# P times V on a balanced array: heads 4 and 5 spread over four column groups, and one matmul chunk of the second MLP layer put ahead of the projection

## The chip, the cores and the metric

The kernel runs on one core of a Trainium2 chip. The core has five engines that run on their own and meet at semaphores: TensorE (PE, matmuls; the profile shows its weight loads apart, as PEld), VectorE (DVE), ScalarE (ACT), GpSimd (POOL) and SyncE (SP, which only issues DMAs here). Matmuls read SBUF and write PSUM; DVE and ACT carry results out of PSUM. The metric is the device time of one execution in microseconds, lower is better.

## What is computed

One Swin block on a batch of 16 images of 56 x 56 pixels with 192 channels, in float32: layer norm, shifted windows of 7 x 7 pixels, attention with 6 heads of 32 channels, projection, residual, layer norm, and an MLP with a hidden width of 768.

```python
xn = layernorm(x, ln1_w, ln1_b)
xs = jnp.roll(xn, shift=(-3, -3), axis=(1, 2))
xw = ...                                  # 1024 windows of 49 tokens
q, k, v = split(xw @ qkv_w + qkv_b)       # 6 heads of 32 channels
attn = softmax(einsum('bhqd,bhkd->bhqk', q, k) * scale)
o = einsum('bhqk,bhkd->bhqd', attn, v)    # P times V
x = x + unroll(o @ proj_w + proj_b)
h = gelu(layernorm(x, ln2_w, ln2_b) @ mlp_w1 + mlp_b1)
x = x + (h @ mlp_w2 + mlp_b2)
```

## The kernel before

The work is cut into 128 groups. A group is one row of 8 windows of one image, 392 tokens, and its 8 windows form 4 pairs. All engines run one loop over the groups, each with its own hand-written order (`body`), and the loop is software pipelined: in turn i, PE does the attention of group i, the MLP of group i-1 and the Q and K of group i+1. Large matmuls work on operands split into a high and a low part (zh and zl, oh and ol, gh and gl), so each evacuation from PSUM is two steps: ACT copies the high part out, then DVE subtracts it from the PSUM value to get the low part.

In one turn PE does, in this order: the scores `s` (L832), the transposes `transposes2` (L774, L776), the values `v` (L806 on zh and wqkv), the first MLP layer `mlp1` (L803), the transposed probabilities `turn_probs` (L910), `transposes1` (L766), two chunks of the second MLP layer `mlp2` (L878 to L884), P times V (`pv`, L929), mlp2 chunks 2 and 3 and the high part of chunk 4, the projection `proj` (L806 on oh, ol and wproj), the high part of chunk 5 and the low parts of 4 and 5, Q and K of the next group (`qk`, L803 on wqkv), and the transposes of the MLP result `turn_result` (L895, L898). A high part of a chunk is three matmuls (L878, L879, L880), a low part two (L883, L884).

P times V: for each of 4 pairs, 6 heads and 2 windows of the pair there is one matmul of a 49 x 32 stationary operand (values) and 49 moving columns (transposed probabilities), 48 in all. A float32 matmul stands in the trace as two weight loads and two matmuls, so 96 of each. The window of the pair sets the row half of the array (partitions 0 to 48 or 64 to 112), the head sets one of four groups of 32 columns, and so there are eight parts. Before the change, head h goes to column group h % 4: groups 0 and 1 carry two heads, groups 2 and 3 one. In program matmuls that is 8 for each of four parts and 4 for each of the other four; in trace records 16 and 8. The outputs of heads 0 to 3 lie in the first half of two PSUM banks, those of heads 4 and 5 in the second half, on 64 partitions.

After `pv`, ACT copies the high parts into oh: one instruction for heads 0 to 3 (L740, 128 partitions), one for heads 4 and 5 (L741, 64 partitions). DVE then makes the low parts (L584 into ol, L586 into the second half of oh), and `proj` waits for both (`ol_ready`). DVE goes on with the low parts of the next group's input (L433, L436), adds the residual to the projection (L530, one for each half, each after `proj_done`), takes statistics of it (L413, L418), moves queries out (L458), adds the narrow part of the MLP result (L548, `yTb_ready`), normalises (L426) and adds the second residual (L540, `yo_done`). `turn_result` on PE waits for L548 of the same turn; `v` of the next turn waits for L540, as `wait(pe, yo_done, 2, i - 2, 2)`, because the values go to the two PSUM banks that L540 reads. `s` waits for the copies of Q and K by ACT (L646, L649).

Of the kernel before, what the change touches and what calls it, by code (L numbers as in the profile page):

```python
# [7 lines left out]
ALU = mybir.AluOpType  # L8
ACT = mybir.ActivationFunctionType
AX = mybir.AxisListType  # L10
F32 = mybir.dt.float32
# [3 lines left out]
WS, SHIFT, HEADS = 7, 3, 6  # L15
HD = C // HEADS
TOK = WS * WS
# [3 lines left out]
PAIRS = WIN // 2  # L21
# [5 lines left out]
M = WIN * TOK  # L27
# [8 lines left out]
PROB_BLOCKS = ((0, 0), (0, 1), (4, 1), (1, 0), (1, 1), (5, 1), (2, 0), (2, 1), (4, 0), (3, 0), (3, 1), (5, 0))  # L36
# [3 lines left out]
def swin_kernel(nc, x, ln1_w, ln1_b, qkv_w, qkv_b, proj_w, proj_b, ln2_w, ln2_b, mlp_w1, mlp_b1, mlp_w2,  # L40
                mlp_b2, out):
    with ExitStack() as ctx:
# [42 lines left out]
        vt = sb("vt", [PAIR + 1, PAIRS, C])  # L85
# [4 lines left out]
        pt = sb("pt", [128, 2 * TILES, TOK])  # L90
        oh = sb("oh", [128, 2, M], F32R)
        ol = sb("ol", [128, M], F32R)
# [28 lines left out]
        PV = 2  # L121
# [59 lines left out]
        def wait(eng, s, per_group, group, k):  # L181

            v = group * per_group + k
            if not isinstance(v, int) or v > 0:
                eng.wait_ge(s, v)
# [26 lines left out]
        def by_window_parity(cols):  # L212

            return cols.rearrange("p (u w c) -> p w u c", w=2, c=WS)

        def outputs(part):

            return ps[:, PV:PV + 2, part * M // 2:(part + 1) * M // 2].rearrange("p w (u c) -> p w u c", c=WS)

        def half_of(t, half):  # L220

# [186 lines left out]
        def _(dve):  # L408
# [151 lines left out]
            def body(i, parity):  # L560
                prev = i - 1
                if attends(i):
                    scores(i, 0)
                if feeds(i):
                    low_wide2(prev)
                if attends(i):
                    scores(i, 1)
                if feeds(i):
                    low_narrow2(prev)
                if not feeds(i):  # L570
                    dve.wait_ge(consts_loaded, 16 * NCONST)
                    offset_bias(1, ((128, slice(HID0, HID0 + KC)),))
                if attends(i):
                    row_sums(i, 0)
                    row_sums(i, 1)
                    normalise(dve, i, 1)
                if more(i):
                    apply1(i + 1, 1 - parity)
                if more(i + 1) and attends(i):
                    stats1(i + 2, parity)  # L580
                if attends(i):

                    wait(dve, oh_ready, 2, i, 2)
                    dve.tensor_tensor(by_window_parity(ol[:, :]), outputs(0), by_window_parity(oh[:, 0, :]).bitcast(F32),  # L584
                                      ALU.subtract).then_inc(ol_ready, 1)
                    dve.tensor_tensor(by_window_parity(oh[64:128, 1, :]), outputs(1)[0:64],  # L586
                                      by_window_parity(oh[0:64, 1, :]).bitcast(F32), ALU.subtract).then_inc(ol_ready, 1)
                if more(i):
                    low_parts1(i + 1)
                if not feeds(i):  # L590
                    low_mlp_weights()
                if attends(i):

                    wait(dve, xb_done, 1, i, 1)
                    wait(dve, yo_done, 2, i - 2, 2)
                    wait(dve, z2_done, 1, i - 1, 1)
                    for half in range(2):
                        residual(i, parity, half)
                    wait(dve, x2_done, 2, i, 2)
                    norm_stats(x2[:, parity, :, :], st2, mv2, bn2, mv2_done, i)  # L600
                    if more(i):
                        queries_45(i + 1)
                if feeds(i):
                    narrow_result(prev)
                if attends(i):
                    z2_pieces = []
                    for h in range(BLOCKS // 2):
                        z2_pieces += [(z2[:, h, 0:C], 2 * h, slice(0, C)), (z2[:, h, C:C + B], 2 * h + 1, slice(A, C)),
                                      (z2[:, h, C + B:2 * C], 2 * h + 1, slice(0, A))]
                    wait(dve, t2_done, 1, i - 1, 1)  # L610
                    norm_apply(x2[:, parity, :, :], mv2, rs2, z2_pieces, i, mv2_done, rs2_done, z2_done)
                if feeds(i):
                    result(prev, 1 - parity)
# [5 lines left out]
        def _(act):  # L619
# [87 lines left out]
            def body(i, parity):  # L707
                prev = i - 1
                if feeds(i):
                    wait(act, h_done, KC, prev - 1, KC)  # L710
                    high_parts2(prev)
                if attends(i):
                    exponential(i, 0)
                    values(i)
                    exponential(i, 1)
                if feeds(i):
                    wait(act, spare_done, 2, prev - 1, 2)
                    act.activation(spare[:, :], ident[0:1, 0:1], ACT.Gelu).then_inc(spare_done, 1)
                    for m in range(4):
                        gelu(prev, m)  # L720
                    high_gelu(prev, 0)
                    high_gelu(prev, 1)
                if attends(i):
                    wait(act, pv_done, 1, i - 1, 1)
                    for half in range(2):
                        wait(act, pt_done, 2, i, half + 1)
                        act.activation(half_of(pt, half).rearrange("p (r s) q -> p r s q", r=2),  # L727
                                       ps[:, TP[half]:TP[half] + 2, 0:384]
                                       .rearrange("p r (s t) -> p r s t", t=64)[:, :, :, 0:TOK],
                                       ACT.Copy).then_inc(pt_ready, 1)  # L730
                if feeds(i):
                    high_gelu(prev, 2)
                    gelu(prev, 4)
                    gelu(prev, 5)
                    for m in range(3, KC):
                        high_gelu(prev, m)
                if attends(i):
                    wait(act, proj_done, 2, i - 1, 2)
                    wait(act, pv_done, 1, i, 1)
                    act.activation(by_window_parity(oh[:, 0, :]), outputs(0), ACT.Copy).then_inc(oh_ready, 1)  # L740
                    act.activation(by_window_parity(oh[0:64, 1, :]), outputs(1)[0:64], ACT.Copy).then_inc(oh_ready, 1)  # L741
                if more(i):
                    wait(act, v_done, 1, i, 1)
                    high_parts1(i + 1)
                if feeds(i):
                    wait(act, spare_done, 2, prev, 1)
                    act.activation(spare[:, :], ident[0:1, 0:1], ACT.Exp).then_inc(spare_done, 1)
                    narrow_result(prev)
                    wide_result(prev)
                else:  # L750
                    high_mlp_weights()
                    act.wait_ge(bias_ready, 2)
                if more(i):
                    keys_45(i + 1)
                    heads_0123(i + 1)
# [5 lines left out]
        def _(pe):  # L761
# [153 lines left out]
            def pv(i):  # L915

                wait(pe, pt_ready, 2, i, 2)
                pe.nop(nofuse=True)
                for pp in range(2):
                    for e in range(2):  # L920
                        for heads in ((0, 1, 4, 2), (3, 5)):
                            for h in heads:
                                b, p = PROB_BLOCKS.index((h, pp)), 2 * pp + e
                                cols = slice(32 * (h % 4), 32 * (h % 4) + 32)
                                for w in range(2):
                                    r = slice(64 * w, 64 * w + TOK)
                                    dst = ps[cols, PV + w, h // 4 * M // 2:(h // 4 + 1) * M // 2]\
                                        .rearrange("p (r q c) -> p q r c", q=PAIRS, c=WS)[:, p]
                                    last = pe.matmul(dst, vt[r, p, HD * h:HD * h + HD], pt[r, 2 * b + e, :], start=True,  # L929
                                                     stop=True)  # L930
                last.then_inc(pv_done, 1)

            def proj(i):
# [27 lines left out]
            def body(i, parity):  # L961
# [28 lines left out]
                    pv(i)  # L990
                if feeds(i):
                    mlp2(prev, (2, 3), (2, 3))
                    mlp2(prev, (4,), ())
                if attends(i):
                    proj(i)
                if feeds(i):
                    mlp2(prev, (5,), (4, 5))
                if more(i):
                    qk(i + 1, (2,))
                    qk(i + 1, (1, 0))  # L1000
# [24 lines left out]
```

## Time and profile before

| | us |
|---|---|
| median of 3 runs | 3045.3 |
| lowest and highest | 3044.94, 3047.61 |
| the profiled execution, its own time | 3046.47 |
| its span in the trace | 3044.7 |

| engine | busy us | share of the span |
|---|---|---|
| PE | 2996.3 | 98% |
| PEld | 2857.5 | 94% |
| DVE | 2376.0 | 78% |
| ACT | 2306.3 | 76% |
| POOL | 1483.4 | 49% |

The profile shows one execution. A busy share is the time in which an engine has an instruction running; matmuls overlap and their ends are modelled, so a PE that is never idle in this measure can still start its next matmul late. The starts of weight loads show that better: each load starts as soon as the matmul ahead of it has started, unless it waits for a semaphore.

### The profile page before, as it was taken

To read this page: it belongs to the slowest core of one execution; us is meant where nothing else is said; L and a number is where in the kernel's file an instruction comes from. 1 tells how busy PE (TensorE), PEld (TensorE's weight loads), DVE (VectorE), ACT (ScalarE), POOL (GpSimd) and SP (SyncE) were. 2 spreads that over 40 slices of the span, in tenths; PEclk is the share of its full clock that TensorE was granted. 3 is DMA by queue.
4 is the path that set the end of the run, shared out by engine and by line. 5 is a ranking of instruction groups with operands and counts; after the bars stand their busy time and mean duration, and the time that the engine had idled before them with its cause. 6 is when DMAs were issued, how large, how long until landed. Compare 5 with 4: busy or idle time off the path is not lost.

```text
span 3044.7 us, 114197 instructions
## 1 busy us (share of the span) xinstructions
PE 2996.3 (98%) x43444; PEld 2857.5 (94%) x43444; DVE 2376.0 (78%) x6416; ACT 2306.3 (76%) x4493; POOL 1483.4 (49%) x1550
## 2 busy tenths in 40 slices
PE   5999999999999999999999999999999999999998
PEld 5999999999999999999999999999999999999997
DVE  4778877887887788788778878877887788788775
ACT  2777777777777777777777777777777777777776
POOL 1454455445445544544554454445445544544553
PEclk7999999999999999999999999999999999999999
DMA  1000100010011001001100100010010001001100
GB/s 46 26 24 24 29 26 24 25 30 24 24 27 28 24 24 31 25 24 27 29 24 24 30 26 24 26 29 24 24 29 26 24 26 29 24 24 28 28 24 17
DMA packets 112145, 79.78 MB, mean 26 GB/s; under 512 B 10128, under 2 KB 111602, under 8 KB 112114
## 3 DMA queue, kind: packets, MB, share of 16 engines
q1 hardware_dynamic: 112114, 79.35, 9.7%
q8 instruction: 22, 0.36, 0.1%
q14 instruction: 9, 0.07, 0.0%
HBM read 40.78 MB, written 38.54 MB: 26 GB/s over the span
## 4 chain that ended last, share of the span: by engine, by line
PE 97%; SPq 1%; DVE 1%; ACT 0%; issue 0%; POOL 0%; DMA 0%; DVEq 0%; POOLq 0%; ACTq 0%
PE ps L803 35%; PE ps L806 16%; PE ps L878 6%; PE ps L910 5%; PE ps L832 5%; PE ps L883 5%; PE ps L929 4%; PE ps L884 4%; PE ps L880 4%; PE ps L879 4%; PE ps L766 3%; PE ps L774 2%; PE ps L895 2%; PE ps L898 1%; SPq L286 1%; PE ps L776 1%
## 5 line engine op out<-in xcount | busy, mean ns | idle before, releaser
L383 POOL TENSOR_TENSOR gl<-g,gh 128x392 fp32r<-128x392 f32 x768 | 789.5, 1050 | 251.6 <-ACT gh L668 251.3
L803 PE MATMUL ps<-zh,w 128*128 128x392 f32 x3072 | 715.0, 348 | 0.6 <-ACT zh L630 0.6
L803 PEld LDWEIGHTS ps<-zh,w 128*128 128x128 f32 x3072 | 533.9, 189 | 31.4 <-ACT zh L630 0.8
L263 POOL TENSOR_TENSOR prob<-prob,rcp 128x588 f32<-128x588 f32 x128 | 152.2, 1189 | 537.0 <-DVE rcp L558 537.0
L413 DVE BATCH_NORM_STATS2 st<-xin 98x6 f32<-98x192 f32 x512 | 145.8, 348 | 328.1 <-DMA xin<-in_x 327.9
L662 ACT ACTIVATE g<-ps,biasf 128x392 f32<-128x392 f32 x768 | 389.3, 574 | 3.1 <-PE ps L803 3.0
L366 POOL TENSOR_TENSOR xb<-xin,projbv 98x768 f32<-98x768 f32 x128 | 234.5, 1832 | 296.2 <-DVE z L426 266.2
L803 PE MATMUL ps<-zh,wqkv 128*128 128x400 f32 x1536 | 378.1, 355 | 0.0
L668 ACT ACTIVATE gh<-g 128x392 fp32r<-128x392 f32 x768 | 365.1, 533 | 0.0
L803 PEld LDWEIGHTS ps<-zh,wqkv 128*128 128x128 f32 x1536 | 289.9, 190 | 2.5
L806 PE MATMUL ps<-wqkv,zh 128*114 128x192 f32 x2048 | 289.5, 269 | 0.4 <-issue 0.4
L878 PE MATMUL ps<-gh,w2h 128*128 128x392 f32 x768 | 288.8, 376 | 0.2 <-ACT pt L727 0.2
L680 ACT ACTIVATE yn<-ps,b 64x392 f32<-64x392 f32 x128 | 74.7, 583 | 279.0 <-PE ps L884 279.0
L376 POOL TENSOR_TENSOR rs<-ve,mhalf 98x4 f32<-98x4 f32 x256 | 259.8, 1015 | 20.1
L374 POOL TENSOR_TENSOR ve<-mv,eps 98x4 f32<-98x4 f32 x256 | 51.7, 202 | 445.4 <-DVE mv L418 445.4
L883 PE MATMUL ps<-gl,w2h 128*128 128x392 f32 x768 | 262.8, 342 | 0.1
L803 PE MATMUL ps<-zl,w 128*128 128x392 f32 x768 | 262.6, 342 | 0.0
L806 PEld LDWEIGHTS ps<-wqkv,zh 128*114 128x114 f32 x2048 | 257.2, 181 | 5.5 <-issue 0.5
L884 PE MATMUL ps<-gl,w2s 128*128 128x392 f32 x768 | 261.8, 341 | 0.0
L880 PE MATMUL ps<-gh,w2s 128*128 128x392 f32 x768 | 261.7, 341 | 0.0
L879 PE MATMUL ps<-gh,w2l 128*128 128x392 f32 x768 | 260.7, 339 | 0.0
L806 PE MATMUL ps<-wproj,oh 128*98 128x192 f32 x2048 | 251.3, 253 | 2.3 <-DVE oh L586 2.3
(105 smaller groups left out, 7234.2 us busy)
## 6 DMA issues: line engine op xcount, KB each, us to landing
xin<-in_x SPq DMA_DIRECT2D x128, 147.0 KB
out<-yo SPq DMA_DIRECT2D x128, 147.0 KB
xin<-in_x SPq DMA_DIRECT2D x128, 71.2 KB
out<-yo SPq DMA_DIRECT2D x128, 71.2 KB
xin<-in_x SPq DMA_DIRECT2D x128, 54.8 KB
out<-yo SPq DMA_DIRECT2D x128, 54.8 KB
xin<-in_x SPq DMA_DIRECT2D x128, 18.8 KB
out<-yo SPq DMA_DIRECT2D x128, 18.8 KB
```

The source lines that it names most:

```text
L366: pool.tensor_tensor(xb[:, parity, :, :], xin[:, parity, :, :], projbv[:, :].unsqueeze(1).broadcast_to([PART, BLOCKS, C]), ALU.add)\
L376: pool.tensor_tensor(rs[:, :], ve[:, :], mhalf[:, :], ALU.pow).then_inc(rs_done, 1)
L383: pool.tensor_tensor(gl[:, m, :], g[:, m, :], gh[:, m, :].bitcast(F32), ALU.subtract)\
L662: act.activation(g[:, m, :], ps[:, H[m], 0:M], ACT.Gelu, bias=biasf[:, HID0 + m:HID0 + m + 1])\
L668: act.activation(gh[:, m, :], g[:, m, :], ACT.Copy).then_inc(gh_done, 1)
L803: last = pe.matmul(dst, cols(w, part), act_ if zh is zh2 else windows(act_, WIDE, EVEN), start=(n == 0), stop=(n == 4))
L806: last = pe.matmul(dst, act_[:, tokens], cols(w, part), start=(n == 0), stop=(n == 4))
L878: pe.matmul(wide, w2h[:, k, :], gh[:, k, :], start=(k == 0), stop=False)
L879: pe.matmul(wide, w2l[:, k, :], gh[:, k, :], start=False, stop=False)
L880: pe.matmul(narrow, w2s[:, k, :], gh[:, k, :], start=(k == 0), stop=False)
L883: pe.matmul(wide, w2h[:, k, :], gl[:, k, :], start=False, stop=(k == KC - 1))
L884: last = pe.matmul(narrow, w2s[:, k, :], gl[:, k, :], start=False, stop=(k == KC - 1))
```

## The change

Three edits.

1. In `pv`, heads 4 and 5 of even pairs stay on column groups 0 and 1, those of odd pairs go to groups 2 and 3. Each of the eight parts then gets 6 program matmuls, 12 in trace records. The order within `pv` is changed too: for each two pairs, heads 0 to 3 of the one, heads 0 to 3 of the other, and then heads 4 and 5 of both. The number and shape of the matmuls stay.
2. The outputs of heads 4 and 5 now lie on 128 partitions, half as wide. They are still brought to the same place in oh for the projection, so the copy L741 becomes two copies (one for each parity of pairs, 64 partitions x 196 elements), and so does the subtraction L586. DVE waits for three copies in place of two.
3. The high part of mlp2 chunk 5 moves from behind `proj` to ahead of it.

```diff
--- before.py
+++ after.py
@@ -213,9 +213,17 @@
 
             return cols.rearrange("p (u w c) -> p w u c", w=2, c=WS)
 
-        def outputs(part):
-
-            return ps[:, PV:PV + 2, part * M // 2:(part + 1) * M // 2].rearrange("p w (u c) -> p w u c", c=WS)
+        def outputs_0123():
+
+            return ps[:, PV:PV + 2, 0:M // 2].rearrange("p w (u c) -> p w u c", c=WS)
+
+        def outputs_45(e):
+
+            return ps[64 * e:64 * e + 64, PV:PV + 2, M // 2:M // 2 + M // 4].rearrange("p w (u c) -> p w u c", c=WS)
+
+        def pairs_of_parity(cols, e):
+
+            return cols.rearrange("p (u e w c) -> p e w u c", e=2, w=2, c=WS)[:, e]
 
         def half_of(t, half):
 
@@ -580,11 +588,14 @@
                     stats1(i + 2, parity)
                 if attends(i):
 
-                    wait(dve, oh_ready, 2, i, 2)
-                    dve.tensor_tensor(by_window_parity(ol[:, :]), outputs(0), by_window_parity(oh[:, 0, :]).bitcast(F32),
-                                      ALU.subtract).then_inc(ol_ready, 1)
-                    dve.tensor_tensor(by_window_parity(oh[64:128, 1, :]), outputs(1)[0:64],
-                                      by_window_parity(oh[0:64, 1, :]).bitcast(F32), ALU.subtract).then_inc(ol_ready, 1)
+                    wait(dve, oh_ready, 3, i, 3)
+                    dve.tensor_tensor(by_window_parity(ol[:, :]), outputs_0123(),
+                                      by_window_parity(oh[:, 0, :]).bitcast(F32), ALU.subtract).then_inc(ol_ready, 1)
+                    for e in range(2):
+                        hi, lo = slice(64 * e, 64 * e + 64), slice(64 - 64 * e, 128 - 64 * e)
+                        last = dve.tensor_tensor(pairs_of_parity(oh[lo, 1, :], e), outputs_45(e),
+                                                 pairs_of_parity(oh[hi, 1, :], e).bitcast(F32), ALU.subtract)
+                    last.then_inc(ol_ready, 1)
                 if more(i):
                     low_parts1(i + 1)
                 if not feeds(i):
@@ -737,8 +748,10 @@
                 if attends(i):
                     wait(act, proj_done, 2, i - 1, 2)
                     wait(act, pv_done, 1, i, 1)
-                    act.activation(by_window_parity(oh[:, 0, :]), outputs(0), ACT.Copy).then_inc(oh_ready, 1)
-                    act.activation(by_window_parity(oh[0:64, 1, :]), outputs(1)[0:64], ACT.Copy).then_inc(oh_ready, 1)
+                    act.activation(by_window_parity(oh[:, 0, :]), outputs_0123(), ACT.Copy).then_inc(oh_ready, 1)
+                    for e in range(2):
+                        act.activation(pairs_of_parity(oh[64 * e:64 * e + 64, 1, :], e), outputs_45(e), ACT.Copy)\
+                           .then_inc(oh_ready, 1)
                 if more(i):
                     wait(act, v_done, 1, i, 1)
                     high_parts1(i + 1)
@@ -916,18 +929,27 @@
 
                 wait(pe, pt_ready, 2, i, 2)
                 pe.nop(nofuse=True)
+                def head_of(h, pp, e):
+
+                    b, p = PROB_BLOCKS.index((h, pp)), 2 * pp + e
+                    for w in range(2):
+                        r = slice(64 * w, 64 * w + TOK)
+                        if h < 4:
+                            dst = ps[32 * h:32 * h + 32, PV + w, 0:M // 2].rearrange("p (r q c) -> p q r c", q=PAIRS, c=WS)[:, p]
+                        else:
+                            c0 = 64 * e + 32 * (h - 4)
+                            dst = ps[c0:c0 + 32, PV + w, M // 2:M // 2 + M // 4]\
+                                .rearrange("p (r q c) -> p q r c", q=2, c=WS)[:, pp]
+                        last = pe.matmul(dst, vt[r, p, HD * h:HD * h + HD], pt[r, 2 * b + e, :], start=True, stop=True)
+                    return last
+
                 for pp in range(2):
                     for e in range(2):
-                        for heads in ((0, 1, 4, 2), (3, 5)):
-                            for h in heads:
-                                b, p = PROB_BLOCKS.index((h, pp)), 2 * pp + e
-                                cols = slice(32 * (h % 4), 32 * (h % 4) + 32)
-                                for w in range(2):
-                                    r = slice(64 * w, 64 * w + TOK)
-                                    dst = ps[cols, PV + w, h // 4 * M // 2:(h // 4 + 1) * M // 2]\
-                                        .rearrange("p (r q c) -> p q r c", q=PAIRS, c=WS)[:, p]
-                                    last = pe.matmul(dst, vt[r, p, HD * h:HD * h + HD], pt[r, 2 * b + e, :], start=True,
-                                                     stop=True)
+                        for h in range(4):
+                            head_of(h, pp, e)
+                    for e in range(2):
+                        for h in range(4, HEADS):
+                            last = head_of(h, pp, e)
                 last.then_inc(pv_done, 1)
 
             def proj(i):
@@ -990,11 +1012,11 @@
                     pv(i)
                 if feeds(i):
                     mlp2(prev, (2, 3), (2, 3))
-                    mlp2(prev, (4,), ())
+                    mlp2(prev, (4, 5), ())
                 if attends(i):
                     proj(i)
                 if feeds(i):
-                    mlp2(prev, (5,), (4, 5))
+                    mlp2(prev, (), (4, 5))
                 if more(i):
                     qk(i + 1, (2,))
                     qk(i + 1, (1, 0))
```

In the order of the changed kernel line numbers are 8 to 14 higher (L878 becomes L891, L883 L896, L806 L819, L929 L943, L584 L592, L586 L596). PE between P times V and the next Q and K, first before (two chunks of mlp2, of which the last row of chunk 3 is shown, then the high part of chunk 4, the projection, the high part of chunk 5):

```order
L884 MATMUL ps<-gl,w2s 128x392
L878 MATMUL ps<-gh,w2h 128x392
L879 MATMUL ps<-gh,w2l 128x392
L880 MATMUL ps<-gh,w2s 128x392
L806 MATMUL ps<-wproj,oh 98x192 x2
L806 MATMUL ps<-wproj,ol 98x192
...
L806 MATMUL ps<-wproj,oh 98x192 x2
L878 MATMUL ps<-gh,w2h 128x392
L879 MATMUL ps<-gh,w2l 128x392
L880 MATMUL ps<-gh,w2s 128x392
L883 MATMUL ps<-gl,w2h 128x392
```

The same place now:

```order
L897 MATMUL ps<-gl,w2s 128x392
L891 MATMUL ps<-gh,w2h 128x392
L892 MATMUL ps<-gh,w2l 128x392
L893 MATMUL ps<-gh,w2s 128x392
L891 MATMUL ps<-gh,w2h 128x392
L892 MATMUL ps<-gh,w2l 128x392
L893 MATMUL ps<-gh,w2s 128x392
L819 MATMUL ps<-wproj,oh 98x192 x2
L819 MATMUL ps<-wproj,ol 98x192
...
L819 MATMUL ps<-wproj,oh 98x192 x2
L896 MATMUL ps<-gl,w2h 128x392
```

Three matmuls moved from behind the projection to ahead of it; nothing else on PE changed places but the order inside `pv`.

DVE around the low parts of the attention output, before:

```order
L413 BN_STATS st<-xin 98x6 x4
L418 BN_AGGR mv<-st 98x2 x4
L584 TENSOR_TENSOR ol<-ps,oh 128x2x28x7
L586 TENSOR_TENSOR oh<-ps,oh 64x2x28x7
L433 TENSOR_TENSOR zl<-ps,zh 128x8x49
L436 TENSOR_TENSOR zh<-ps,zh 64x8x49
L530 TENSOR_TENSOR x<-ps,xb 98x384 x2
```

And now:

```order
L421 BN_STATS st<-xin 98x6 x4
L426 BN_AGGR mv<-st 98x2 x4
L592 TENSOR_TENSOR ol<-ps,oh 128x2x28x7
L596 TENSOR_TENSOR oh<-ps,oh 64x2x14x7 x2
L441 TENSOR_TENSOR zl<-ps,zh 128x8x49
L444 TENSOR_TENSOR zh<-ps,zh 64x8x49
L538 TENSOR_TENSOR x<-ps,xb 98x384 x2
```

One subtraction became two of half the width; the place is the same.

## Rows read from the trace of the kernel before

**Rows 1.** The page: busy us, share of the span, instructions.

```profile
PE 2996.3 (98%) x43444; PEld 2857.5 (94%) x43444; DVE 2376.0 (78%) x6416; ACT 2306.3 (76%) x4493; POOL 1483.4 (49%) x1550
```

**Rows 2.** DVE in order of time: start, length, what, idle before.

```profile
1502.44 0.57 DVE L584 TENSOR_TENSOR ol<-ps,oh 128x392 fp32r<-128x392 f32 x1 [0.86 <-ACT oh L741]
1503.03 0.56 DVE L586 TENSOR_TENSOR oh<-ps,oh 64x392 fp32r<-64x392 f32 x1
...
1504.23 0.57 DVE L436 TENSOR_TENSOR zh<-ps,zh 64x392 fp32r<-64x392 f32 x1
1504.94 0.56 DVE L530 TENSOR_TENSOR x<-ps,xb 98x384 f32<-98x384 f32 x1
1505.73 0.56 DVE L530 TENSOR_TENSOR x<-ps,xb 98x384 f32<-98x384 f32 x1 [0.24 <-PE ps L806]
1506.33 1.14 DVE L413 BATCH_NORM_STATS2 st<-x 98x6 f32<-98x192 f32 x4
...
1507.98 0.85 DVE L458 TENSOR_SCALAR qB<-ps,biasf 64x200 f32<-64x200 f32 x2
1508.76 0.71 DVE L548 TENSOR_TENSOR yTb<-ps,yn 64x196 f32<-64x196 f32 x2
1509.50 1.63 DVE L426 TENSOR_SCALAR z<-x,mv,rs 98x192 f32<-98x192 f32 x6
1511.05 1.02 DVE L540 TENSOR_TENSOR yo<-ps,x 98x512 f32<-98x512 f32 x2
```

**Rows 3.** Weight loads (PEld) in order of time, ahead of projection, transposes and values.

```profile
1503.39 0.19 PEld L880 LDWEIGHTS ps<-gh,w2s 128*128 128x128 f32 x1
1503.65 0.27 PEld L806 LDWEIGHTS ps<-wproj,oh 128*98 128x98 f32 x2
...
1509.08 0.38 PEld L803 LDWEIGHTS ps<-zh,wqkv 128*128 128x128 f32 x2
1509.54 0.46 PEld L895 LDWEIGHTS ps<-ident,yT 128*98 128x98 f32 x4
...
1511.85 0.23 PEld L776 LDWEIGHTS ps<-ident,z 98*128 98x128 f32 x2
1512.12 0.28 PEld L806 LDWEIGHTS ps<-wqkv,zh 128*114 128x114 f32 x2
```

**Rows 4.** The transposes' load in a later turn, DVE and then PEld.

```profile
2506.29 0.71 DVE L548 TENSOR_TENSOR yTb<-ps,yn 64x196 f32<-64x196 f32 x2
...
2507.07 0.46 PEld L895 LDWEIGHTS ps<-ident,yT 128*98 128x98 f32 x4
```

**Rows 5.** The chain of waits in order of time: start, length, what.

```profile
1500.32 1.07 PE ps L929 x73
...
1506.07 0.18 PE ps L880
...
1510.47 1.15 PE ps L832 x71
```

**Rows 6.** P times V in the first turn and in a later one, PE in order of time.

```profile
58.29 1.62 PE L929 MATMUL ps<-pt,vt 49*32 49x49 f32 x96
...
1500.25 1.14 PE L929 MATMUL ps<-pt,vt 49*32 49x49 f32 x96
```

**Rows 7.** Windows of those two: stretch, us, busy PE, busy PEld, granted clock, DMA share, GB/s.

```profile
58.29:59.63 1.34, 1.34 (x95) 1.34 (x96) 0.50 0.31 69
1500.25:1501.31 1.06, 1.06 (x96) 1.00 (x96) 1.00 0.00 0
```

**Rows 8.** ACT in order of time: the copies after P times V, and a pair of half-width copies.

```profile
1501.48 0.53 ACT L740 ACTIVATE oh<-ps 128x392 fp32r<-128x392 f32 x1 [0.29 <-PE ps L929]
1501.90 0.50 ACT L741 ACTIVATE oh<-ps 64x392 fp32r<-64x392 f32 x1
...
1512.70 0.67 ACT L633 ACTIVATE zh<-ps 64x196 fp32r<-64x196 f32 x2
```

## The prediction

> **What bounds the kernel now.** The page comes first: PE is busy 98% of the span, its weight loads 94%, DVE 78%, ACT 76% [rows 1]. Read alone, it says that PE is the bound and the rest follows. The busy time of PE can't show a matmul that starts late, so I went to the starts of the weight loads and set them beside DVE in order of time [rows 2, 3]. Three loads a turn start late, and each has an instruction of DVE that ends just before it.
>
> The projection: the load ahead of it starts at 1503.39 and loads come every 0.18 us there, so it could start at 1503.57; it starts at 1503.65, and DVE's last low part (L586) ends at 1503.03 + 0.56 = 1503.59. It is 0.08 us late. The transposes of the MLP result: two loads of L803 from 1509.08 take 0.38, so 0.19 apart, and the next could start at 1509.46; it starts at 1509.54, and L548 ends at 1508.76 + 0.71 = 1509.47. Again 0.08 late. The values of the next turn: L540 ends at 1511.05 + 1.02 = 1512.07, the load starts at 1512.12, 0.27 after the last pair of L776 loads began and so about 0.1 later than a load that waits for nothing [rows 2, 3]. A turn 1000 us later has the same distance: L548 ends at 2506.29 + 0.71 = 2507.00, the load starts at 2507.07 [rows 4]. So these are waits that bind, each small.
>
> They belong to one loop. DVE's second residual add starts at 1505.73 after 0.24 of idling on PE, when the projection is done. From there DVE works without a pause that matters: 1506.33, 1507.98, 1508.76, 1509.50, 1511.05, to 1512.07 [rows 2]. That is 3.74 us to the end of L548 and 6.34 to the end of L540, whatever PE does meanwhile. PE spends the 3.74 on what stands behind the projection: mlp2 chunks, Q and K. It fills them all but 0.08. **The work between the projection and the transposes is PE's cover for DVE, and it is used up on both sides.** A turn is as long as PE's way from the values to the end of the projection, plus DVE's way from there to the values.
>
> **The change part by part.** There are 127 turns with all the pieces (a first without an MLP, a last without attention); one takes 23.2 us.
>
> The moved chunk. Three matmuls go from behind the projection to ahead of it, 0.18 each [rows 5], 0.54 us. Ahead of the projection they first fill its wait of 0.08. The rest, 0.46, makes the projection end later. Behind it PE comes to the transposes 0.54 earlier, and L548 is not a bit earlier: it comes 3.74 after the second residual add starts, and that add waits for the projection. So the wait at L895 grows from 0.08 to 0.62, and the turn by 0.54 - 0.08 = 0.46 us. The moved loads need the high part of chunk 5, which ACT makes before it copies the output of P times V; ACT even idles 0.29 before that copy [rows 8], so this waits for nothing. Late next, once the transposes wait longer: the scores, the next MLP's transposes and the values. The values wait for L540, which stays 2.60 behind L548 (1512.07 - 1509.47), as before; the scores' wait for the copies of Q and K only becomes easier.
>
> The copies in two. ACT's second copy, L741, takes 0.50; a pair of half width, L633, takes 0.67 [rows 8]: +0.17. DVE's L586 takes 0.56; a pair of half width, L548, takes 0.71 [rows 2]: +0.15. The access patterns are different (runs of 7 elements), so the ends are 0 and, if each half cost a full one, 0.50 + 0.56 = 1.06; I take 0.32, the pair rows being of the same size in elements. They lie on the way from P times V to the projection. That way had no slack (0.08 too long); with 0.54 us more PE work beside it there is 0.46, and 0.32 fits. **The split costs nothing, but only since the chunk was moved.** Queued behind the two subtractions are L433, L436 and the first residual add. L436 would end at 1504.80 + 0.32, the add at 1504.94 goes with the projection to + 0.46, so 0.28 of idling remains there; nobody waits.
>
> P times V. The chain gives it 1.07 us [rows 5]. Its fullest parts have 16 of the 96 matmuls, and after the change 12. If the fullest part sets the time, it falls to 12/16 of 1.07 = 0.80: a gain of 0.27. Against that, two sets of rows. The scores have the same number, 96 records, evenly over eight parts, 12 each, and take 1.15 [rows 5]; their stationary operand has 64 columns for 32, but if balance were the key they would not be slower than the uneven one. And the first turn ran at half clock (0.50, that is 1.2 GHz, against 1.00 or 2.4 GHz later) [rows 7]: P times V took 1.62 there and 1.14 at full clock [rows 6], 1.4 times and not 2. So at full clock most of it is not bound by the array's own streaming, but by something that does not follow that clock; 96 pairs in 1.07 are 11 ns a pair, the scores' 12 ns. I take the pace at which pairs are handed to the array as the bound, which balance does not change. The bounds are a gain of 0.27 and a loss of 0.08 (the scores' pace); I take a gain of 0.03, near to the scores' row, for the spells in which a part is asked for twice in a row.
>
> In TensorEngine Tiling (Array Packing) the Trainium skill says, under Key Properties, that tiles operate independently and can load weights and multiply in parallel. By that rule the fullest part is the bound and the gain is the 0.27 above; the half-clock rows and the scores speak against it as the bound at full clock, and it stands as a rival below.
>
> Sum: 0.54 - 0.08 - 0.03 = 0.43 us a turn, x127 = 55 us. On the span of 3044.7 that is 3100, on the execution's own 3046.5 it is 3101, on the median of 3045.3 it is 3100. **I forecast 3100 us, 1.8% slower.**
>
> **Rivals.**
>
> A. The fullest part of the array is the bound. P times V gains 0.27 in place of 0.03: (0.46 - 0.27) x 127 = 24 us, 3069. Still slower: the gain in P times V is real, but less than what the moved chunk exposes. For it: 16 turns of the fullest part in 1.07 are 67 ns each, a plausible load and stream. Against it: the scores and the half clock. Chance 0.20.
>
> B. It gets faster. PE is the bound after all, and the order behind the projection is free: the DVE work has slack that the trace doesn't show. Then the 0.08 at the projection goes, with 0.03 to 0.27 of P times V: 0.11 x 127 = 14 us, 3031, down to 0.35 x 127 = 44 us, 3001. It decides at the transposes: it holds if DVE's way to L548 shrinks by over 0.46 when PE runs ahead. Against it: loads that start 0.07 after L548 a thousand us apart, and a DVE without pauses from the second add on. Chance 0.08.
>
> C. It stays within the noise: A, and DVE's way gets some 0.2 shorter. 3045. Chance 0.03.
>
> D. The split copies cost far more than the pairs suggest, up to a full copy each, 1.06. Then the projection waits for L596 again: 1.06 - 0.46 = 0.60 more, (0.43 + 0.60) x 127 = 131 us, 3176. It decides from 0.46. The pair rows speak against it: 0.32. Chance 0.05.
>
> **How the numbers follow.** The forecast has 0.64, A 0.20, B 0.08, C 0.03, D 0.05. The predicted time is 3100. The range takes in A with its bound, 3067, and at the upper end P times V at the scores' pace: (0.46 + 0.08) x 127 = 69, 3114. These hold 0.84 less what falls just outside. A measurement of this kernel can tell some 0.2%, 6 us, from no change. Faster by more than that: B, 0.08. Within it: 0.03. Slower: 0.64 + 0.20 + 0.05 = 0.89.
>
> **What would show each step right or wrong.** The chunk: the load of L908 (the transposes) would start some 0.6 after the last load of Q and K in place of 0.27, still 0.07 behind DVE's narrow result, and PE's busy share would fall for the first time by a visible amount. The second residual add would still be followed by 3.74 us to the end of the narrow result. The projection: its first load would come 0.18 behind the load ahead of it, and DVE's last low part would have ended 0.1 to 0.2 earlier. P times V: 1.04 in the chain, where A says 0.80. The copies: 0.67 for ACT's pair, 0.71 for DVE's. I am wrong if the load of the transposes starts without a wait, or if the turn is 23.2 us or less; the step that failed would then be the length of DVE's way.

## The result and the profile after

The changed kernel took 3109.07 us in the median of 4 runs (3107.56 to 3110.56), the kernel before beside it 3046.45 (3044.94 to 3047.64): a ratio of 1.0208, 95% interval 1.0196 to 1.0220. It is slower, by 63 us or 0.49 us a turn. I had forecast 3100, in a range of 3067 to 3114.

The first lines of the page of the changed kernel, as [rows 1]:

```profile
span 3108.8 us, 114514 instructions
...
PE 3024.9 (97%) x43444; PEld 2852.8 (92%) x43444; DVE 2396.4 (77%) x6544; ACT 2344.9 (75%) x4621; POOL 1482.8 (48%) x1550
```

PE's busy time rose by 29 us with the same 43444 instructions, while the weight loads' fell by 5 us, to 92% of the span from 94%. In Perfetto Trace Analysis, under Identifying the Most-Contended Engine, the Trainium skill says that the matmul busy share is not a good measure of how close a kernel is to its limit, and names the busy share of weight loads (and the share of peak arithmetic) in its place. This trace agrees: the time grew by 2%, the loads' share fell by two points and the matmuls' by one.

DVE in order of time in one turn of the changed kernel, from the low parts to the second residual of the MLP result, as [rows 2]:

```profile
1486.26 0.57 DVE L592 TENSOR_TENSOR ol<-ps,oh 128x392 fp32r<-128x392 f32 x1 [1.00 <-ACT oh L753]
1486.85 0.73 DVE L596 TENSOR_TENSOR oh<-ps,oh 64x196 fp32r<-64x196 f32 x2
...
1489.09 0.56 DVE L538 TENSOR_TENSOR x<-ps,xb 98x384 f32<-98x384 f32 x1 [0.31 <-PE ps L819]
1489.89 0.56 DVE L538 TENSOR_TENSOR x<-ps,xb 98x384 f32<-98x384 f32 x1 [0.24 <-PE ps L819]
...
1492.91 0.71 DVE L556 TENSOR_TENSOR yTb<-ps,yn 64x196 f32<-64x196 f32 x2
...
1495.21 1.01 DVE L548 TENSOR_TENSOR yo<-ps,x 98x512 f32<-98x512 f32 x2
```

The second residual add starts at 1489.89 and the narrow result (L556, L548 before) ends at 1492.91 + 0.71 = 1493.62, 3.73 later; the second residual of the MLP ends at 1496.22, 6.33 later. Before it was 3.74 and 6.34: DVE's way kept its length to 0.01 us.

The weight loads of the same turn, as [rows 3]:

```profile
1487.56 0.19 PEld L893 LDWEIGHTS ps<-gh,w2s 128*128 128x128 f32 x1
1487.73 0.34 PEld L819 LDWEIGHTS ps<-wproj,oh 128*98 128x98 f32 x2
...
1492.72 0.38 PEld L816 LDWEIGHTS ps<-zh,wqkv 128*128 128x128 f32 x2
1493.69 0.39 PEld L908 LDWEIGHTS ps<-ident,yT 128*98 128x98 f32 x4 [0.59 <-issue]
...
1496.27 0.28 PEld L819 LDWEIGHTS ps<-wqkv,zh 128*114 128x114 f32 x2
```

The load ahead of the projection (1487.73) comes 0.17 behind the one ahead of it and waits for nothing; the low part L596 had ended at 1487.58. The load of the transposes could start at 1493.10 and starts at 1493.69, 0.59 late and 0.07 after L556 ended. In [rows 3] it was 0.08 late, with the same 0.07. The values' load starts 0.05 after the second residual (L548) ended, as before (L540 there).

The copies on ACT, as [rows 8]:

```profile
1485.11 0.53 ACT L751 ACTIVATE oh<-ps 128x392 fp32r<-128x392 f32 x1 [0.26 <-PE ps L943]
1485.52 0.70 ACT L753 ACTIVATE oh<-ps 64x196 fp32r<-64x196 f32 x2
```

The pair of half-width copies takes 0.70 on ACT (I took 0.67), and 0.73 on DVE (0.71).

The chain of waits of the changed kernel in the same turn, and the projection of the next one, as [rows 5]:

```profile
1483.98 1.03 PE ps L943 x67
...
1488.07 1.78 PE ps L819 x20
...
1493.46 0.27 issue
1493.72 0.61 PE ps L908 x4
...
1496.36 2.16 PE ps L819 x20
...
1511.77 1.78 PE ps L819 x20
```

P times V takes 1.03 (1.07 before, 1.04 forecast). From its start to the projection's first matmul it is 1488.07 - 1483.98 = 4.09 us. The turn is 1511.77 - 1488.07 = 23.70 us, against 23.19 before (below). And the chain now has a piece with no work in it ahead of L908. Beside the 0.27 of that piece the four transposes take 0.61, where they took 0.44 before, so PE stands still there for 0.44 us, less than the 0.59 by which the load is late. The values (L819 at 1496.36) take 2.16, where they took 2.10.

The same chain in the kernel before, further rows of the turn of [rows 5]:

```profile
1503.73 0.18 PE ps L880
1503.91 1.79 PE ps L806 x20
...
1506.96 2.85 PE ps L803 x15
1509.81 0.44 PE ps L895 x4
...
1512.27 2.10 PE ps L806 x20
...
1527.10 1.79 PE ps L806 x20
```

Here the projection's matmuls begin at 1503.91, exactly when the last one ahead of them has had its 0.18. From P times V to the projection it was 1503.91 - 1500.32 = 3.59 us, so that way grew by 0.50. That is 0.54 for the three matmuls less 0.04 for P times V, and nothing given back by the wait at the projection.

### The profile page after: what moved, and what is told of

Read it like the earlier page. It is cut to its first block, busy times and chain, and to the rows that moved or that the text cites. A ratio compares the mean times of both kernels' runs of the same rounds, so it can differ in the third digit from the quotient of the medians.

```text
span 3108.8 us, 114514 instructions
## 1 busy us (share of the span) xinstructions
PE 3024.9 (97%) x43444; PEld 2852.8 (92%) x43444; DVE 2396.4 (77%) x6544; ACT 2344.9 (75%) x4621; POOL 1482.8 (48%) x1550
## 4 chain that ended last, share of the span: by engine, by line
PE 96%; issue 1%; SPq 1%; DVE 1%; ACT 0%; POOL 0%; DMA 0%; DVEq 0%; POOLq 0%; ACTq 0%
PE ps L816 34%; PE ps L819 16%; PE ps L891 5%; PE ps L923 5%; PE ps L845 5%; PE ps L896 5%; PE ps L897 4%; PE ps L893 4%; PE ps L892 4%; PE ps L943 4%; PE ps L779 3%; PE ps L908 2%; PE ps L787 2%; PE ps L911 1%; SPq L294 1%
## 5 line engine op out<-in xcount | busy, mean ns | idle before, releaser
L819 PE MATMUL ps<-wqkv,zh 128*114 128x192 f32 x2048 | 291.3, 270 | 0.5 <-issue 0.5
L891 PE MATMUL ps<-gh,w2h 128*128 128x392 f32 x768 | 286.6, 373 | 0.2 <-ACT pt L738 0.2
L641 ACT ACTIVATE zh<-ps 128x392 fp32r<-128x392 f32 x128 | 63.6, 497 | 285.2 <-PE ps L789 285.2
L819 PEld LDWEIGHTS ps<-wqkv,zh 128*114 128x114 f32 x2048 | 258.7, 182 | 13.7 <-issue 0.7
L896 PE MATMUL ps<-gl,w2h 128*128 128x392 f32 x768 | 265.8, 346 | 0.2 <-POOL gl L391 0.2
L819 PE MATMUL ps<-wproj,oh 128*98 128x192 f32 x2048 | 250.5, 253 | 2.7 <-DVE oh L596 2.7
```

The source lines that it names most:

```text
L819: last = pe.matmul(dst, act_[:, tokens], cols(w, part), start=(n == 0), stop=(n == 4))
L891: pe.matmul(wide, w2h[:, k, :], gh[:, k, :], start=(k == 0), stop=False)
L896: pe.matmul(wide, w2h[:, k, :], gl[:, k, :], start=False, stop=(k == KC - 1))
```

## The experiments

Two ways make up the theory. PE's way goes from the values to the end of the projection. DVE's way goes from there to the transposes and the next values, and what PE does in the meantime is free as long as it is shorter. A tie is a place where a weight load of PE starts right after the instruction of DVE that it waits for. The rivals: that PE alone is the bound, so that a place in its order costs nothing; that the copies in two cost the time; and, for P times V, that the fullest part of the array is its bound. Line numbers are those of each kernel. The runs were made in three sets; the kernel before had a median of 3045.16 us in the first (15 runs), 3042.30 in the second (15) and 3045.74 in the third (13).

### Each edit alone

**e1_no_chunk_move**: the changed kernel with the chunk back behind the projection.

```diff
-                    mlp2(prev, (4, 5), ())
+                    mlp2(prev, (4,), ())
                 if attends(i):
                     proj(i)
                 if feeds(i):
-                    mlp2(prev, (), (4, 5))
+                    mlp2(prev, (5,), (4, 5))
```

> The changed kernel with the high part of mlp2 chunk 5 back behind the projection; balance, order and split copies stay. Theory (loop of PE's way up to the end of the projection plus DVE's way from there to the transposes and the values): the copies in two have lengthened the way from P times V to the projection by some 0.38 us (ACT 0.20, DVE 0.18 by the trace of after), and without the chunk ahead of it PE has nothing to do in that time. The projection's load comes some 0.46 us late instead of 0.08, the turn is 0.38 - 0.04 = 0.34 us longer than before, 3089 us. Rival 1 (the copies are hidden, all of the loss is the chunk): 3040 us, a little faster than before by the 0.04 of P times V. Rival 2 (the loss is in the copies, not in the chunk): 3109 us, as the changed kernel.

Measured: 3085.17 us, ratio 1.0128 (1.0111 to 1.0145). DVE and the loads in one turn:

```profile
1499.41 0.74 DVE L596 TENSOR_TENSOR oh<-ps,oh 64x196 fp32r<-64x196 f32 x2
...
1499.57 0.19 PEld L893 LDWEIGHTS ps<-gh,w2s 128*128 128x128 f32 x1
1500.20 0.25 PEld L819 LDWEIGHTS ps<-wproj,oh 128*98 128x98 f32 x2 [0.45 <-DVE oh L596]
```

The load could have started at 1499.75; it starts 0.45 later, just behind the last low part (L596), where 0.46 was expected. The copies in two do cost time where nothing covers them: 40 us in all, so neither rival holds. In the changed kernel the moved chunk covers them, and costs more than they would. The late load does not count in full: from the start of P times V to the end of the projection the chain has 5.70 us here and 5.38 before, and with the 0.04 that P times V gained PE stands still for 0.36 of the 0.45.

**e2_chunk_only**: the kernel before with the chunk moved and nothing else, the same diff the other way round.

> The kernel before with the chunk alone moved ahead of the projection; P times V and the copies as before. Theory: PE's way to the end of the projection grows by three matmuls, 0.54 us, and the wait ahead of the transposes by the same; the late load ahead of the projection cost no matmul time and gives nothing back. 0.54 x 127 = 69 us, 3114 us. By the working of the prediction 0.08 of it would come back: 3103 us. Rival (PE's order behind the projection is free): 3046 us or a little less.

Measured: 3111.11 us, ratio 1.0218 (1.0201 to 1.0235), 66 us more than before. DVE's narrow result and the loads around it in one turn, and the chain of waits there:

```profile
1491.81 0.71 DVE L548 TENSOR_TENSOR yTb<-ps,yn 64x196 f32<-64x196 f32 x2
...
1491.60 0.38 PEld L803 LDWEIGHTS ps<-zh,wqkv 128*128 128x128 f32 x2
1492.59 0.39 PEld L895 LDWEIGHTS ps<-ident,yT 128*98 128x98 f32 x4 [0.61 <-issue]
...
1492.33 0.29 issue
```

The transposes' load starts 0.61 late, again 0.07 after the narrow result ended. One moved chunk of three matmuls, 0.54 us, makes the whole loss and a little more: 66 us is 0.52 a turn. The working that gave 0.08 of it back asked for 3103. The work on PE is the same as before, only its place is not, so PE alone is not the bound.

### DVE's way taken away

**e4_short_dve**: the changed kernel with three of four statistics instructions of the second layer norm left out.

```diff
-                for p in range(BLOCKS):
+                short = st is st2
+                for p in range(1 if short else BLOCKS):
                     last = dve.bn_stats(st[:, p, :], src[:, p, :])
 ...
-                    last = dve.bn_aggr(mv[:, p, :], st[:, p, :])
+                    last = dve.bn_aggr(mv[:, p, :], st[:, 0 if short else p, :])
```

> The changed kernel with three of the four statistics instructions of the second layer norm left out (all four blocks use the first block's statistics), which takes some 0.8 us out of DVE's way from the projection to the transposes and touches nothing on PE. Theory: the wait of 0.6 us ahead of the transposes goes, and the one ahead of the values, and PE is the bound: 23.70 - 0.54 - 0.09 = 23.07 us a turn, 3029 us. Rival (PE alone is the bound, or the loss is in the copies): 3109 us, no change.

Measured: 3035.10 us, ratio 0.9968 (0.9956 to 0.9981). DVE and the loads of one turn:

```profile
1499.57 0.56 DVE L539 TENSOR_TENSOR x<-ps,xb 98x384 f32<-98x384 f32 x1 [0.24 <-PE ps L820]
...
1502.05 0.71 DVE L557 TENSOR_TENSOR yTb<-ps,yn 64x196 f32<-64x196 f32 x2
...
1504.34 1.02 DVE L549 TENSOR_TENSOR yo<-ps,x 98x512 f32<-98x512 f32 x2
...
1502.40 0.38 PEld L817 LDWEIGHTS ps<-zh,wqkv 128*128 128x128 f32 x2
1502.83 0.49 PEld L909 LDWEIGHTS ps<-ident,yT 128*98 128x98 f32 x4
...
1505.41 0.28 PEld L820 LDWEIGHTS ps<-wqkv,zh 128*114 128x114 f32 x2
```

DVE's way to the narrow result shrank from 3.73 to 3.19 us, that to the second residual from 6.33 to 5.79, and 74 us went, with PE's program unchanged. Some 0.8 us of instructions left DVE but its way got only 0.54 shorter, because DVE now has to wait for PE: the trace puts 0.27 of idling ahead of the queries (L467), until the matmuls that make them (L817) are done. The loads still come 0.07 after 1502.76 and 0.05 after 1505.36. At the transposes this costs nothing any more (0.44 in the chain, as before), the values take 2.06, and the 3029 us that I expected were not reached.

### P times V

**e3_order_only**: the kernel before with the new order, all of heads 4 and 5 still on two column groups.

```diff
-                for pp in range(2):
-                    for e in range(2):
-                        for heads in ((0, 1, 4, 2), (3, 5)):
-                            for h in heads:
...
+                for h, pp, e in [(h, pp, e) for pp in range(2) for hs in ((0, 1, 2, 3), (4, 5)) for e in range(2) for h in hs]:
...
```

> The kernel before with the new order inside P times V, but heads 4 and 5 all on column groups 0 and 1, so that the fullest parts still have 16 of 96 records; one copy each. If P times V is bound by the pace at which pairs are handed over, and the 0.04 us of after came from its order, it takes 1.03 us in the chain here too: 3040 us. If balance gave it, or the fullest part is the bound, it takes 1.07 or more: 3045 us or more.

Measured: 3044.70 us, ratio 0.9999 (0.9989 to 1.0008). P times V in its chain of waits:

```profile
1497.93 1.09 PE ps L926 x80
```

It takes 1.09: the new order alone is a little slower than the old one in the trace (0.02 us a turn, too little to show in the kernel's time), and the balance is worth 1.09 - 1.03 = 0.06 us beside it. Before this run I had put the 0.04 down to the order; it came from the balance.

**e5_by_head**: the kernel before with P times V head by head, so that a part of the array is asked for again and again.

```diff
+                for h, pp, e in [(h, pp, e) for h in range(HEADS) for pp in range(2) for e in range(2)]:
...
```

> The kernel before with P times V in the order head by head: the 16 records of a head go to the same two parts of the array (the two row halves of one column group), one after the other. If a part can take its next record only some 41 ns after the last (49 moving columns, twice, at 2.4 GHz), a head takes 8 x 41 = 0.33 us, P times V 1.97 us in place of 1.07, and the kernel 3045 + 0.9 x 128 = 3160 us. If there is no such limit and only the handing over of pairs counts, P times V stays at 1.07 and the kernel at 3045 us.

Measured: 3103.82 us, ratio 1.0202 (1.0187 to 1.0218). Its chain of waits:

```profile
1503.93 1.54 PE ps L926 x85
```

1.54 us, neither 1.07 nor 1.97. The 0.47 more stand ahead of the projection and are paid in full, as the theory asks: 0.47 x 128 = 60 us, against 62 measured. When the same parts are asked for again and again, the four records of a head and pair, which go in twos to two parts, take 1.54 / 24 = 0.064 us on average: at most 32 ns a record. There is a limit of the part, but at 32 ns the 16 records of the fullest part need 0.51 us, half of the 1.07 of the kernel before. So the fullest part is not what bounds P times V there; it costs a little where its records come close together.

The starts of the weight loads say more. In the changed kernel, from the tenth of the 24 groups of four records on, 12 of the 14 distances to the next group are 34 ns and two are 45 (medians over the turns), whichever parts the groups go to. In e5 they lie between 36 and 92 ns. So where the parts change often enough the records come at an even 8 to 9 ns each; the 11 ns that 1.03 / 96 gives also hold 0.17 us from the last load to the first matmul behind P times V.

### Versions that use the cover

**b1_low1_behind**: the kernel before, with two matmuls moved the other way.

```diff
-                    mlp2(prev, (0, 1), (0, 1))
+                    mlp2(prev, (0, 1), (0,))
 ...
-                    mlp2(prev, (5,), (4, 5))
+                    mlp2(prev, (5,), (1, 4, 5))
```

> The kernel before with the low part of mlp2 chunk 1 (two matmuls, 0.36 us) moved from ahead of P times V to behind the projection. By the theory of the two ways PE's way up to the projection gets shorter by up to 0.29 (ACT idles that long ahead of its copy), DVE's way is then no longer the bound, the wait of 0.09 at the values goes, and some 0.07 of it comes back at the projection, since ACT is late: 0.02 to 0.09 x 127, 3034 to 3043 us. Rival (PE alone is the bound and its order is free): 3045 us.

Measured: 3040.30 us, ratio 0.9992 (0.9983 to 1.0001). PE's way got shorter, but DVE's got longer. DVE in order of time:

```profile
1503.40 0.56 DVE L530 TENSOR_TENSOR x<-ps,xb 98x384 f32<-98x384 f32 x1 [0.24 <-PE ps L806]
...
1505.98 0.85 DVE L458 TENSOR_SCALAR qB<-ps,biasf 64x200 f32<-64x200 f32 x2 [0.36 <-PE ps L803]
...
1509.04 1.01 DVE L540 TENSOR_TENSOR yo<-ps,x 98x512 f32<-98x512 f32 x2
```

DVE now idles 0.36 ahead of the queries (L458), because the matmuls that make them stand behind the moved ones; its way to the end of L540 is 6.65 us in place of 6.34. PE's way is 0.36 shorter and DVE's 0.31 longer, which leaves 0.05 us a turn or 6 us; 2 were measured, within the interval of no change.

**b6_dve_swap_only**: the kernel before with the queries (L458) behind the narrow result (L548) on DVE.

```diff
-                    if more(i):
-                        queries_45(i + 1)
                 if feeds(i):
                     narrow_result(prev)
+                if attends(i) and more(i):
+                    queries_45(i + 1)
```

> The kernel before with DVE's narrow result ahead of the queries and nothing else. L548 ends some 0.8 us earlier, but the values still wait for L540, which comes no earlier: by the theory nothing is gained, 3042 us. Rival (the tie of the transposes cost 0.08 of PE's time a turn): 3032 us.

Measured: 3032.70 us, ratio 0.9953 (0.9936 to 0.9970), where I expected nothing. DVE and the values' load of one turn, and the transposes and the values in its chain of waits:

```profile
1499.22 0.56 DVE L530 TENSOR_TENSOR x<-ps,xb 98x384 f32<-98x384 f32 x1 [0.24 <-PE ps L806]
...
1501.35 0.69 DVE L548 TENSOR_TENSOR yTb<-ps,yn 64x196 f32<-64x196 f32 x2
...
1504.44 1.02 DVE L540 TENSOR_TENSOR yo<-ps,x 98x512 f32<-98x512 f32 x2
...
1505.51 0.27 PEld L806 LDWEIGHTS ps<-wqkv,zh 128*114 128x114 f32 x2
...
1503.29 0.44 PE ps L895 x4
...
1505.75 2.01 PE ps L806 x20
```

The swap made DVE's way to the end of L540 6.24 us, 0.10 shorter, and the turn got shorter by 13 us / 127 = 0.10 us. The rule held, my guess that the way would keep its length did not. The rival's number, 3032, came out too, but not its reason: the transposes' load now has 0.90 us of slack behind L548, and yet the transposes take 0.44 in the chain, as before, so their late load had cost nothing. The gain lies at the values, 2.01 in place of 2.10. The narrow result now starts 0.08 before the record of the statistics ahead of it ends, where the queries started 0.03 after it; why the order does that was not followed up.

**b3_low1_and_dve_swap** is b1 with that swap. **b7_low1_and_act** is b1 with the copies of the attention output ahead of the high part of chunk 5 on ACT. **b4_act_first** has all three:

```diff
-                    for m in range(3, KC):
+                    for m in range(3, KC - 1):
                         high_gelu(prev, m)
 ...
                     act.activation(by_window_parity(oh[0:64, 1, :]), outputs(1)[0:64], ACT.Copy).then_inc(oh_ready, 1)
+                if feeds(i):
+                    high_gelu(prev, KC - 1)
```

> b4 without the edit on ACT: the low part of mlp2 chunk 1 behind the projection, and DVE's narrow result ahead of the queries. If the tie of L548 to the transposes was what b1 still waited for, this takes most of b4's gain, 3028 us; if ACT's lateness ahead of the copies was, it stays at b1's 3040 us.

> b4 without the edit on DVE: the low part of mlp2 chunk 1 behind the projection, and ACT's copies of the output of P times V ahead of the high part of chunk 5. If ACT's lateness is what held b1 back, this takes most of b4's gain, 3028 us; if the tie of L548 was, it stays near 3040 us.

> As b1, and ACT copies the output of P times V before the high part of mlp2 chunk 5 instead of after it, and DVE makes the narrow part of the MLP result before it moves the queries out, so that the transposes' tie gets 0.8 us of slack. All three ties with DVE loosen: 0.09 x 127 = 11 us gained, 3034 us; PE is then the bound. Rival: 3045 us.

**b5_after_act_first** is the changed kernel with the same edits on ACT and DVE, and the low parts of chunks 0 and 1 behind the projection.

> The changed kernel with the low parts of mlp2 chunks 0 and 1 (four matmuls, 0.72 us) moved from ahead of P times V to behind the projection, and the two edits of b4 on ACT and DVE. PE's way up to the projection is 0.6 to 0.7 us shorter than in the changed kernel, which takes back all of its loss and the 0.09 at the values, and the 0.04 of P times V stays: 3109 - 0.6 x 127 = 3033, bounded below by PE's own work at 3028 us. Rival (the split copies or the balance cost time of their own): over 3045 us.

| kernel | us, median | ratio to before | 95% interval |
|---|---|---|---|
| b3 | 3027.68 | 0.9935 | 0.9919 to 0.9952 |
| b7 | 3040.75 | 0.9982 | 0.9972 to 0.9991 |
| b4 | 3024.34 | 0.9937 | 0.9924 to 0.9951 |
| b5 | 3026.32 | 0.9945 | 0.9931 to 0.9959 |

b3 has all of b4's gain and b7 little of it: DVE's way was the thing to shorten, and the edit on ACT can be left out. DVE's way is 6.24 us in b3 and 6.67 in b7, and in b3 the values' load starts 0.42 after L540 ended: that tie is loose, and PE sets the turn. Of b3's 0.15 us a turn 0.09 lie at the values and 0.05 at the first MLP layer; what made the latter was not followed up. b4 and b5 came out 10 and 7 us below what was expected, and below the 3028 that I had taken for PE's own floor. b5 takes the changed kernel from 3109 to 3026 without touching P times V or the split copies. It has the better P times V, and still does not beat b3 and b4, whose intervals overlap with its own. It differs from them in the split copies and in PE's order too, so it does not isolate the balance; it only shows no gain from it. b3, with two edits, beats both kernels, by 0.65% and 2.7%; b6, with one, has 0.47% of it.

## Why the prediction was right, and where its size was off

**The loop of two ways.** Right. DVE's way kept its length (3.73 and 6.33 against 3.74 and 6.34), the load of the transposes started 0.07 behind it, and the turn became longer by what stood newly on PE's way up to the projection. e2 (PE's order alone, 66 us) and e4 (DVE's way alone, 74 us) show it from both sides.

**The moved chunk.** Its 0.54 was right; the 0.08 that should come back at the projection was not. I read a late weight load as lost time. The chain of the kernel before shows no gap between L880 (1503.73, 0.18) and L806 (1503.91): the load starts 0.08 late there, and the projection's matmuls still begin exactly when the one ahead of them has had its 0.18. The same holds for L895 before, which follows L803 at 1509.81 with no gap. Of a later load a part stays hidden: 0.45 late made a gap of 0.36 at the projection (e1), 0.59 late one of 0.44 at the transposes. The step that was mis-sized is this one term: 0 in place of 0.08, which is 10 us. With it the sum is 0.54 - 0.04 = 0.50 us a turn, 64 us, against 63 measured. e2 with 66 us, where 58 would have come with the refund and 69 without, agrees. Of the three late loads in the prediction only the third, that of the values, cost time before: 2.10 in the chain against 2.01 in b6, 0.09 us a turn. It is also the one that sets the length of the turn, 6.34 us behind the second residual add before and 6.33 now, which is why nothing of the 0.50 came back. That of the 0.50 some 0.44 appear at the transposes and 0.06 at the values (2.16) is only where PE spends the wait.

One sign was written down wrongly: I asked for the transposes' load to start some 0.6 after the last load of Q and K in place of 0.27. It had to be 0.27 + 0.54 = 0.81 by my own working; 0.78 was measured. The 0.6 is the delay against a load that waits for nothing (0.59).

**The copies in two.** ACT 0.70 and DVE 0.73 against 0.67 and 0.71. The cover that the moved chunk gives was enough: DVE's low part ended 0.15 before the projection's load. e1 shows the price without cover, a load 0.45 late. Rival D is out.

**P times V.** 1.03 where I said 1.04 and rival A 0.80. The gain of 0.03 was picked between bounds that lay 0.35 apart, so its closeness is in part luck; e3 shows that the balance made it, and the order took 0.02 of it back. The rule of the Trainium skill that tiles run independently (TensorEngine Tiling (Array Packing), Key Properties) is not contradicted: e5 gives a part 32 ns a record, and eight parts together take one every 11. But at 32 ns the fullest part needs 0.51 us, and the P times V of the kernel before takes twice that, so something common to all parts sets most of it; the even 34 ns for four records in the changed kernel fit that. That this is the handing over of pairs, 96 in 1.03 us or 11 ns a pair, is argued from the half-clock turn, the scores and this even pace, and no run isolated it. In TensorE: Matmul & The Clock Gate, under Wait — 56ns, not 53.3ns?, the Trainium skill puts a floor of about 25 ns under the distance of matmul starts. This trace differs, with 11 ns on average.

**The rivals.** A and B fall with the trace of after: the gain of P times V is 0.04, and the transposes and the values do wait. C falls with them.

## What to carry to other kernels

Where one engine is busy for 98% of the time and another at 78% feeds it, look for the stretches in which the second works without a pause from one hand-over to the next: work of the first engine inside such a stretch is free, work outside it is paid. Moving three matmuls out of such a stretch cost 2%, moving two into it and shortening the stretch gained 0.65%, and shortening it alone 0.47%. Such a stretch can hide a wait of its own: when it got shorter (e4), or when more work was put into it (b1), the second engine came to wait for the first (0.27 and 0.36 us ahead of the queries). And a weight load that starts late is a warning, not yet a loss: the loss is the gap between matmuls.

## What the runs showed of the hardware

- P times V, 96 matmul records over eight parts of the array, takes 1.03 us with 12 records in each part, 1.07 or 1.09 with 16 in four of them, and 1.54 when the same two parts are asked for again and again (e5).
- A pair of copies of 64 x 196 elements takes 0.70 us on ACT and 0.73 on DVE, one of 64 x 392 takes 0.50 and 0.56 [rows 8] [rows 2]: the split costs 0.20 and 0.17 us.
- A weight load that waits for DVE starts 0.07 us after L548 ended at the transposes and 0.05 us after L540 at the values, in the kernel before and, under its own line numbers, in the changed one.
- A late weight load costs less than it is late: nothing for 0.08 us, 0.36 for 0.45 (e1), 0.44 for 0.59 (the changed kernel).
- The order of two instructions on DVE (L458 and L548) changed the length of its way by 0.10 us, with the same instructions in it.
